# Writing the unshifted scores of a relative attention in four transfers of 32 rows instead of one of 128

## The chip, the cores and the metric

The kernel is one program on one core of a Trainium2 chip. The metric is device time in microseconds (us), from the start of the program to its end, as a median of several executions. Lower is better. Shares of the span are given against one profiled execution.

## The reference

The program is a chain of four layers on a tensor of 8 x 512 tokens of width 128: a plain attention, a causal attention with a mixture of experts, an attention with relative positions, and a low-rank feed-forward layer. The change touches the third. Cut to what matters there:

```python
def _rel_shift(x):
    B, H, Lq, Lr = x.shape
    xp = jnp.concatenate([jnp.zeros((B, H, Lq, 1), x.dtype), x], axis=-1)
    xp = xp.reshape(B, H, Lr + 1, Lq)
    return xp[:, :, 1:].reshape(B, H, Lq, Lr)[..., Lr - Lq:]
...
AC = jnp.einsum('bhid,bhjd->bhij', q + u_bias[None, :, None, :], k)
BD = jnp.einsum('bhid,hjd->bhij', q + v_bias[None, :, None, :], rp)
BD = _rel_shift(BD)
attn = jax.nn.softmax((AC + BD) * scale, axis=-1)
out = jnp.einsum('bhij,bhjd->bhid', attn, v)
```

There are 16 heads of 8 elements and 512 queries and keys. Row i of BD has to be moved sideways by an amount that grows by one from row to row, before it is added to AC.

## The kernel before

The layer is `phase_relative` (line 2260). It runs NI = 32 steps, one for each of 8 sequences and 4 groups of 4 heads. A step holds 16 tiles of 128 queries x 512 keys, in two halves (c = 0 and 1) of HT = 8 tiles; a buffer index s alternates from step to step. For each half:

- TensorE computes the unshifted scores of 8 tiles side by side (`wide_bank`, L2440) and ScalarE copies them from PSUM to SBUF (`copy_wide`, L2519) into `wide[:, s, c, :]`, 128 partitions x CW = 4448 columns of float32. The scores of a tile take W = 544 columns. Row r of the buffer is needed with a shift that depends on r. The four groups of Q = 32 rows are computed with different starts, `start = W * v + P - Q - Q * a` for group a, so that each group fills 8 x 544 = 4352 of the 4448 columns: from column 96 for the first group, 64, 32 and 0 for the others.
- ScalarE's queue issues the transfer `send` (L2524) that writes the buffer to DRAM (`skew`), all 128 rows with all 4448 columns.
- SyncE's queue waits for that write (`sent`) and issues `fetch` (L2353), which reads it back with a row pitch of CW - 1 = 4447, so that each row comes back shifted by one more than the row before: 128 partitions x 4320 columns into `shifted`.
- VectorE adds the content scores that TensorE made in PSUM (L2574) and subtracts the row maximum (L2582), TensorE turns the tile (L2456), ScalarE takes the exponential (L2540), TensorE multiplies with the values (L2469), and ScalarE copies the sums out (L2530).

The order on each engine is written by hand. In step n the wide scores of step n + 2 are made, copied and sent, one bank behind each tile; `send` stands behind tile 7 and tile 15 in ScalarE's order. SyncE's order in a step is: values of the next step, four stores of sums, fetch of half 1 of step n + 1, fetch of half 0 of step n + 2, then the loads of `qu` and `k` and of `qv` (48 partitions each). A fetch waits for its send, and SyncE issues nothing behind it meanwhile. Before ScalarE overwrites `wide[:, s, c, :]` two steps later it waits for the send that read it (L2546). So a half-step, of which there are 64, asks the transfer queues for one send and one fetch, and every second one for three loads on 48 partitions as well.

Of the kernel before, what the change touches and what calls it, by code (L numbers as in the profile page):

```python
# [13 lines left out]
P = 128  # L14
# [7 lines left out]
NI = NB * NG  # L22
# [11 lines left out]
Q = 32  # L34
TG = G * NT
W = L + Q
HT = TG // 2
CW = HT * W + P - Q
# [2221 lines left out]
def phase_relative(nc, sems, qu_stacks, qv_stacks, k_stacks, v9_in, r_stack, ident_in, skew_dram, ctx_out):  # L2260
# [14 lines left out]
    with ExitStack() as ctx:  # L2275
        def sb(name, shape, dt=F32):
            return ctx.enter_context(nc.sbuf_tensor("r_" + name, shape, dt))


        def sem(name):  # L2280
            return sems.new("r_" + name)
# [10 lines left out]
        wide = sb("wide", [P, 2, 2, CW])  # L2292
# [17 lines left out]
        sent = [[sem(f"sent{s}{c}") for c in range(2)] for s in range(2)]  # L2310
# [13 lines left out]
        def steps(step, eng):  # L2324

            for n in range(NI):
                step(n // STEP, n % STEP, n == 0, min(4, NI - 1 - n))

        def uses(it, j):

            return (STEP // 2) * it + j // 2 + 1

        @block.sync
        def _(sp):
            def load(it, j):
                for dst, src in ((qu, qu_stacks), (k, k_stacks)):
                    sp.dma_start(dst[0:SK, j % 2, :, :],
                                 src.rearrange("b r (g h) t -> b g r h t", h=G)[it, j]).then_inc(loaded[j % 2], 16)

            def load_values(it, j):  # L2340
                sp.dma_start(v9[:, j % 2, :, :], v9_in.rearrange("b p t (g v) -> b g p t v", g=NG)[it, j])\
                    .then_inc(v_loaded[j % 2], 16)

            def load_queries(it, j):
                at = ROWS * (j % 2)
                sp.dma_start(qv[at:at + SK, j % 2, :, 0:L], qv_stacks.rearrange("b r (g h) t -> b g r h t", h=G)[it, j])\
                    .then_inc(qv_loaded[j % 2], 16)

            def fetch(it, j, c):

                sp.wait_ge(sent[j % 2][c], 16 * uses(it, j))
                src = skew_dram[j % 2][c]
                sp.dma_start(shifted[:, j % 2, HT * W * c:HT * W * (c + 1) - Q],  # L2353
                             bass.AP(tensor=src.tensor, offset=src.offset + P - 1, ap=[[CW - 1, P], [1, HT * W - Q]]))\
                    .then_inc(skewed[j % 2][c], 16)

            def after(it, j, by):
                return it + (j + by) // STEP, (j + by) % STEP

            def step(it, j, first, left):  # L2360
                n = STEP * it + j
                if left >= 1:
                    sp.wait_ge(head_done, G * n + 2)
                    load_values(*after(it, j, 1))
                if not first:
                    store(n - 1)
                if left >= 1:
                    if not first:
                        sp.wait_ge(keys_ps, TG * n)
                    fetch(*after(it, j, 1), 1)  # L2370
                if left >= 2:
                    sp.wait_ge(keys_ps, TG * n + HT)
                    fetch(*after(it, j, 2), 0)
                if left >= 2:
                    sp.wait_ge(ac_ps, TG * (n + 1))
                    load(*after(it, j, 2))
                if left >= 4:
                    sp.wait_ge(wide_ps, 2 * NBK * (n + 3))
                    load_queries(*after(it, j, 4))

            def store(n):
                sp.wait_ge(out_sb, n + 2)
                for b in range(NT):
                    sp.dma_start(ctx_out[n, :, :, b * P:(b + 1) * P].rearrange("h r i -> r h i"),
                                 osb[Q * b:Q * b + VW, :, :]).then_inc(stored, 16)

            sp.wait_ge(pad_set, 1)
            load_queries(0, 0)
            load_queries(0, 1)
            sp.wait_ge(pad_set, 2)  # L2390
            sp.dma_start(ident[:, :], ident_in).then_inc(consts, 16)
            for s in range(2):
                sp.dma_start(r[ROWS * s:ROWS * s + SK, :, :, :],
                             r_stack.rearrange("r (o g h) t -> g r o h t", g=2, h=G)[s]).then_inc(r_loaded, 16)
            sp.wait_ge(pad_set, 4)
            load(0, 0)
            load_values(0, 0)
            sp.sem_inc(stored, 64)
            for c in range(2):
                fetch(0, 0, c)  # L2400
            sp.wait_ge(wide_ps, 2 * NBK)
            load_queries(0, 2)
            load(0, 1)
            fetch(0, 1, 0)
            sp.wait_ge(wide_ps, 4 * NBK)
            load_queries(0, 3)
            steps(step, sp)
            store(NI - 1)
            for s in range(2):
                sp.wait_ge(loaded[s], 32 * (NI // 2))  # L2410
                sp.wait_ge(v_loaded[s], 16 * (NI // 2))
                sp.wait_ge(qv_loaded[s], 16 * (NI // 2))
                for c in range(2):
                    sp.wait_ge(sent[s][c], 16 * (NI // 2))
                    sp.wait_ge(skewed[s][c], 16 * (NI // 2))
            sp.wait_ge(r_loaded, 32)
            sp.wait_ge(stored, 64 * (NI + 1))
# [96 lines left out]
        @block.scalar  # L2514
        def _(act):
            def copy_wide(n, s, c, bk):
                act.wait_ge(wide_ps, 2 * NBK * n + NBK * c + bk + 1)
                lo, hi = BANK * bk, min(BANK * bk + BANK, CW)
                act.activation(wide[:, s, c, lo:hi], ps_wide[bk % BANKS][:, 0:hi - lo], ACT.Copy).then_inc(wide_sb, 1)  # L2519

            def send(n, s, c):
                act.wait_ge(wide_sb, 2 * NBK * n + NBK * (c + 1))
                dst = skew_dram[s][c]
                act.dma_start(bass.AP(tensor=dst.tensor, offset=dst.offset, ap=[[CW, P], [1, CW]]),  # L2524
                              wide[:, s, c, :]).then_inc(sent[s][c], 16)

            def take_sums(n):
                act.wait_ge(head_done, G * (n + 1) + 2)
                act.wait_ge(stored, 64 * (n + 1))
                act.activation(osb[:, :, :].rearrange("p h i -> p (h i)"), ps_out[:, :], ACT.Copy)\  # L2530
                    .then_inc(out_sb, 1)

            def step(it, j, first, left):
                n, s = STEP * it + j, j % 2
                for u in range(TG):
                    h, b = u // NT, u % NT
                    if b == 0:
                        act.wait_ge(head_done, G * n + h + 1)
                    act.wait_ge(keys_ps, TG * n + u + 1)
                    act.activation(probs[:, h % 2, :, b * P:(b + 1) * P],  # L2540
                                   ps_keys[u % 2][:, :].rearrange("p (j i) -> p j i", j=NT), ACT.Exp,
                                   scale=SCALE).then_inc(exp_done, 1)
                    if left >= 2:
                        c, bk = u // HT, u % HT
                        if bk == 0:
                            act.wait_ge(sent[s][c], 16 * uses(it, j))  # L2546
                        copy_wide(n + 2, s, c, bk)
                        if bk == HT - 1:
                            copy_wide(n + 2, s, c, HT)
                            send(n + 2, s, c)  # L2550
                    if u == 2 and not first:
                        take_sums(n - 1)

            act.sem_inc(exp_done, 2)
            act.sem_inc(out_sb, 1)
            for n in range(2):
                for c in range(2):
                    for bk in range(NBK):
                        copy_wide(n, n, c, bk)
                    send(n, n, c)  # L2560
            steps(step, act)
            take_sums(NI - 1)

# [146 lines left out]
```

## Time and profile before

| | |
|---|---|
| median of 3 runs | 1982.19 us (1959.62 to 1989.26) |
| profiled execution | 1965.66 us, of which span 1963.9 us |
| relative attention in the span | about 961 to 1850 us |
| sends | 64, 2224 KB each |
| fetches | 64, 2160 KB each |

The span is cut into 40 equal slices of 49 us. The relative attention is slices 20 to 37; in the page's second part it shows as the long row of 9s in the line of the transfer engines. The four layers follow each other with a barrier between, so what a half-step gains or loses there is gained or lost at the end.

### The profile page before, as it was taken

What the parts mean: (1) busy time and instruction counts of PE and PEld (TensorE: products, weight loads), DVE (VectorE), ACT (ScalarE), POOL (GpSimd) and SP (SyncE); (2) the same over time, 40 slices, a digit from 0 to 9 for tenths busy, and PEclk for the clock granted to TensorE, in tenths of its full rate; (3) what the DMA queues carried; (4) which work ended last, traced back from release to release, by engine and by line L of the source; (5) the groups of instructions that cost most, each with busy time, mean ns of one, the idle gap of its engine ahead of it and who ended that gap; (6) DMA issues with size and microseconds to landing.
All of it is one profiled execution on the core that took longest, in us unless ns stands there. A gap on an engine that the chain in (4) does not pass through costs nothing. (4 is left out here: it accounts for less than half of the span.)

```text
span 1963.9 us, 48778 instructions
## 1 busy us (share of the span) xinstructions
PE 1356.6 (69%) x18587; PEld 905.4 (46%) x18775; DVE 1171.8 (60%) x3060; ACT 997.9 (51%) x1988; POOL 449.1 (23%) x756
## 2 busy tenths in 40 slices
PE   6636177777745288745248788787888879888657
PEld 3213044444434277622126555565555556555423
DVE  6943477777345223256317676676767667677636
ACT  4424046666611033223147676676767667776333
POOL 5433235555437600087000000000000000000123
PEclk8867579999955589966679999999999999999868
DMA  8439412222031166548799999999999999999422
GB/s 309 171 103 279 103 43 61 69 62 66 21 101 41 43 179 198 160 136 268 203 339 343 370 377 370 379 379 372 384 378 369 368 379 389 379 377 373 136 66 59
DMA packets 174670, 451.83 MB, mean 230 GB/s; under 512 B 41584, under 2 KB 133776, under 8 KB 157360
## 3 DMA queue, kind: packets, MB, share of 16 engines
q1 hardware_dynamic: 130736, 237.53, 36.7%
q10 hardware_dynamic: 31200, 180.04, 23.3%
q0 software_dynamic: 12512, 31.21, 6.0%
q8 instruction: 151, 2.47, 0.5%
q14 instruction: 71, 0.58, 0.1%
HBM read 222.59 MB, written 225.84 MB: 228 GB/s over the span
## 5 line engine op out<-in xcount | busy, mean ns | idle before, releaser
L2574 DVE CUSTOM_DVE_ANT_0 r_shifted<-r_ps_ac,r_shifted 128x512 f32<-128x512 f32 x512 | 352.0, 688 | 264.1 <-PE r_ps_ac L2449 116.7
L2540 ACT ACTIVATE r_probs<-r_ps_keys 128x512 f32<-128x512 f32 x512 | 309.9, 606 | 215.6 <-PE r_ps_keys L2456 189.4
L2519 ACT ACTIVATE r_wide<-r_ps_wide 128x512 f32<-128x512 f32 (+1 forms) x576 | 330.3, 592 | 84.8 <-PE r_ps_wide L2440 84.6
L2456 PE MATMUL r_ps_keys<-r_ident,r_shifted 128*128 128x128 f32 x2048 | 322.1, 281 | 70.8 <-DMA r_k<-stack 24.4
L2456 PEld LDWEIGHTS r_ps_keys<-r_ident,r_shifted 128*128 128x128 f32 x2048 | 264.1, 145 | 62.9 <-issue 21.5
L2440 PE MATMUL r_ps_wide<-r_r,r_qv 128*32 128x96 bf16 (+12 forms) x6144 | 234.8, 253 | 67.7 <-issue 49.9
L2582 DVE TENSOR_SCALAR r_shifted<-r_shifted,r_mx 128x512 f32<-128x512 f32 x512 | 249.3, 487 | 18.3
L926 ACT ACTIVATE c_probs<-c_ps_keys 128x512 f32<-128x512 f32 (+1 forms) x384 | 174.3, 531 | 140.6 <-PE c_ps_keys L852 140.4
L1135 POOL MEMSET n_zeros<- 128x4 f32 x1 | 0.1, 101 | 906.7 <-POOLq L2275 906.7
L2440 PEld LDWEIGHTS r_ps_wide<-r_r,r_qv 128*32 128x32 bf16 x6144 | 103.6, 97 | 164.5 <-issue 163.7
L2469 PE MATMUL r_ps_out<-r_probs,r_v 128*9 128x128 f32 x4096 | 142.4, 274 | 21.1 <-issue 20.4
L989 DVE TENSOR_REDUCE c_mx_off<-c_ps_rows 128x2 f32<-128x768 f32 (+2 forms) x192 | 120.8, 686 | 53.8 <-PE c_ps_rows L823 53.8
L823 PE MATMUL c_ps_rows<-c_qk 48*128 48x128 bf16 (+2 forms) x896 | 75.6, 254 | 90.9 <-DVE c_mx_off L989 43.7
L2449 PE MATMUL r_ps_ac<-r_k,r_qu 128*128 128x512 bf16 x325 | 130.4, 401 | 5.1 <-issue 4.0
L957 POOL TENSOR_SCALAR_AFFINE_SELECT c_probs<-c_probs 128x256 f32<-128x256 f32 x256 | 98.1, 406 | 149.7 <-ACT c_probs L926 149.2
L2469 PEld LDWEIGHTS r_ps_out<-r_probs,r_v 128*9 128x9 f32 x4096 | 105.1, 91 | 31.7 <-issue 27.3
L2449 PEld LDWEIGHTS r_ps_ac<-r_k,r_qu 128*128 128x128 bf16 x512 | 49.1, 96 | 126.0 <-issue 76.6
L1917 POOL DMA_INDIRECT d_y<-expert_out,x_pos x64 | 68.8, 1075 | 167.5 <-issue 167.4
L852 PE MATMUL c_ps_keys<-c_qk 50*128 50x512 bf16 (+3 forms) x512 | 91.2, 305 | 20.5 <-ACT c_probs L926 20.5
L864 PE MATMUL c_ps_out<-c_probs,c_v 128*9 128x128 f32 x2560 | 84.8, 279 | 4.1 <-POOL c_probs L957 4.1
L983 DVE TENSOR_REDUCE c_mx_on<-c_ps_rows 128x8 f32<-128x1024 f32 x64 | 77.7, 1215 | 16.4 <-PE c_ps_rows L831 16.4
L1792 DVE TENSOR_TENSOR e_gu<-e_silu,e_ps_b 128x512 f32<-128x512 f32 x39 | 26.8, 688 | 87.4 <-PE e_ps_b L1718 87.4
(249 smaller groups left out, 1948.8 us busy)
## 6 DMA issues: line engine op xcount, KB each, us to landing
skew<-r_wide ACTq DMA_DIRECT2D x64, 2224.0 KB, 13.6
r_shifted<-skew SPq DMA_DIRECT2D x64, 2160.0 KB, 13.6
by_expert<-a_blank ACTq DMA_DIRECT2D x4, 4352.0 KB
e_w<-in_L_ffn_w_dram SPq DMA_DIRECT2D x117, 128.0 KB, 2.4
c_qk<-qk_stacks POOLq DMA_DIRECT2D x64, 192.0 KB, 3.7
stack<-d_part SPq DMA_DIRECT2D x96, 128.0 KB
qk_stacks<-b_part SPq DMA_DIRECT2D x48, 128.0 KB, 3.5
qk_stacks<-b_part POOLq DMA_DIRECT2D x48, 128.0 KB, 3.7
```

What stands on the lines that cost most here:

```text
L852: last = pe.matmul(ps[:, to:to + WIDTH[j]], qk[at, s, 1, p, j * P:(j + 1) * P], qk[at, s, 0, p, j * P:L], start=True, stop=True, skip_grou ...
L926: act.activation(probs[:, p, e, at:at + width], ps_keys[f % BANKS][:, 0:width], ACT.Exp, scale=SCALE)\
L957: last = pool.affine_select(blocks, blocks, [[0, 2], [1, P]], ALU.is_ge, zero, base=0, channel_multiplier=-1)
L989: last = dve.tensor_reduce(off[:, :, NT * p + b], ps[:, :, at:at + width], AX_X, ALU.max)
L2440: last = pe.matmul(ps[Q * a:Q * a + Q, frm - lo:to - lo], qv[:, s, h, q0 + one:q0 + one + Q], r[:, g // 2, h, at:at + to - frm], start=Tru ...
L2449: pe.matmul(ps_ac[u % 2][:, :], qu[:, s, h, b * P:(b + 1) * P], k[:, s, h, :], start=True, stop=True)\
L2456: last = pe.transpose(ps_keys[u % 2][:, j * P:(j + 1) * P], shifted[:, s, W * u + j * P:W * u + (j + 1) * P], ident[:, :])
L2469: last = pe.matmul(ps_out[Q * b:Q * b + VW, h * P:(h + 1) * P], v9[:, s, j, h * VW:(h + 1) * VW], probs[:, h % 2, j, b * P:(b + 1) * P], s ...
L2519: act.activation(wide[:, s, c, lo:hi], ps_wide[bk % BANKS][:, 0:hi - lo], ACT.Copy).then_inc(wide_sb, 1)
L2540: act.activation(probs[:, h % 2, :, b * P:(b + 1) * P], ps_keys[u % 2][:, :].rearrange("p (j i) -> p j i", j=NT), ACT.Exp, scale=SCALE).th ...
L2574: dve.tensor_tensor_reduce(out=shifted[:, s, W * u:W * u + L], in0=ps_ac[u % 2][:, :], in1=shifted[:, s, W * u:W * u + L], scale=1.0, scal ...
L2582: dve.tensor_scalar(shifted[:, s, W * u:W * u + L], shifted[:, s, W * u:W * u + L], mx[:, u:u + 1], None, ALU.subtract).then_inc(s_ready, 1)
```

## The change

`send` issues four transfers instead of one. Transfer a takes rows 32a to 32a + 31 of the buffer and only the 4352 columns that the group fills. Each adds 16 to the semaphore `sent`, so the three places that wait on it (the fetch, the reuse of `wide`, and the end of the phase) multiply their number by P // Q = 4. What is fetched, and from where in DRAM, is the same.

```diff
@@ fetch
-                sp.wait_ge(sent[j % 2][c], 16 * uses(it, j))
+                sp.wait_ge(sent[j % 2][c], 16 * (P // Q) * uses(it, j))
@@ send
                 act.wait_ge(wide_sb, 2 * NBK * n + NBK * (c + 1))
                 dst = skew_dram[s][c]
-                act.dma_start(bass.AP(tensor=dst.tensor, offset=dst.offset, ap=[[CW, P], [1, CW]]),
-                              wide[:, s, c, :]).then_inc(sent[s][c], 16)
+                for a in range(P // Q):
+                    lo = P - Q - Q * a
+                    act.dma_start(bass.AP(tensor=dst.tensor, offset=dst.offset + Q * a * CW + lo,
+                                          ap=[[CW, Q], [1, HT * W]]),
+                                  wide[Q * a:Q * a + Q, s, c, lo:lo + HT * W]).then_inc(sent[s][c], 16)
@@ step of ScalarE, before the first copy into wide[:, s, c, :]
-                            act.wait_ge(sent[s][c], 16 * uses(it, j))
+                            act.wait_ge(sent[s][c], 16 * (P // Q) * uses(it, j))
```

No engine but ScalarE has other instructions than before. On ScalarE's queue, in the middle of a step (behind tile 7), stood before:

```order
L2540 ACTIVATE r_probs<-r_ps_keys 128x4x128
L2519 ACTIVATE r_wide<-r_ps_wide 128x512
L2519 ACTIVATE r_wide<-r_ps_wide 128x352
L2524 DMA skew_0<-r_wide 128x4448
L2540 ACTIVATE r_probs<-r_ps_keys 128x4x128
```

and now, with the exponential of the next tile (`r_probs`, now L2543) behind four issues:

```order
L2543 ACTIVATE r_probs<-r_ps_keys 128x4x128
L2519 ACTIVATE r_wide<-r_ps_wide 128x512
L2519 ACTIVATE r_wide<-r_ps_wide 128x352
L2526 DMA skew_0<-r_wide 32x4352 x4
L2543 ACTIVATE r_probs<-r_ps_keys 128x4x128
```

The one issue has become four in a row at the same place, here and behind tile 15 (`skew_1`); nothing has changed places.

## Rows read from the trace of the kernel before

**Rows 1.** The page, second part: 40 slices of the span.

```profile
PE   6636177777745288745248788787888879888657
...
DVE  6943477777345223256317676676767667677636
ACT  4424046666611033223147676676767667776333
...
DMA  8439412222031166548799999999999999999422
```

**Rows 2.** Transfers from 1000 to 1800 us: packets, MB, share of 16 engines; issues.

```profile
DMA packets 48940, 299.41 MB, mean 374 GB/s; under 512 B 20285, under 2 KB 30221, under 8 KB 33101
...
q1 hardware_dynamic: 40028, 158.61, 56.6%
q10 hardware_dynamic: 8783, 138.92, 42.7%
q8 instruction: 100, 1.64, 0.9%
...
skew<-r_wide ACTq DMA_DIRECT2D x61, 2224.0 KB, 13.7
r_shifted<-skew SPq DMA_DIRECT2D x61, 2160.0 KB, 13.5
...
r_qu<-stack SPq DMA_DIRECT2D x30, 192.0 KB, 12.8
```

**Rows 3.** Instructions on the tile skew: ns min/median/max, first and last start.

```profile
L2524 ACTq DMA_DIRECT2D skew<-r_wide x64: 325/326/356, 986.5 to 1799.8; - x64
```

**Rows 4.** Waits from 1100 to 1700 us: us in total, times, longest.

```profile
PEld r_ps_wide L2440 <- issue: 95.5, 389, 3.1
...
PE r_ps_keys L2456 <- DMA r_k<-stack: 16.5, 6, 5.9
```

**Rows 5.** Waits of all engines from 1000 to 1800 us.

```profile
DVE r_shifted L2574 <- DMA r_shifted<-skew: 39.9, 2, 38.0
```

**Rows 6.** Waits of SyncE's queue from 1000 to 1800 us.

```profile
SPq L2351 <- DMA skew<-r_wide: 435.0, 44, 21.8
```

**Rows 7.** Stretches: PE, PEld, DVE, ACT, POOL busy; PEclk; DMA share; GB/s.

```profile
970.00:980.00 10.00, 2.46 (x12) 2.06 (x10) 1.16 (x1) 0.00 (x0) 0.00 (x0) 0.50 1.02 150
...
1226.00:1232.00 6.00, 5.68 (x111) 4.18 (x109) 4.59 (x13) 4.98 (x10) 0.00 (x0) 1.00 0.99 417
...
1400.00:1500.00 100.00, 84.61 (x1504) 57.87 (x1530) 69.70 (x184) 69.32 (x134) 0.00 (x0) 0.95 1.00 371
```

**Rows 8.** Instructions on the tile r_r: its loads from DRAM, 48 partitions each.

```profile
L2393 SPq DMA_DIRECT2D r_r<-r_stack x2: 592/616/640, 967.3 to 968.0; - x2
...
DMA to landing us min/median/max: 8.8/11.1/13.4
```

**Rows 9.** Timeline of ScalarE from 15 to 25 us: issues in a row.

```profile
19.25 0.36 ACTq L396 DMA_DIRECT2D by_expert<-a_blank  x1
...
19.64 0.45 ACTq L396 DMA_DIRECT2D by_expert<-a_blank  x1
...
20.12 2.27 ACTq L396 DMA_DIRECT2D by_expert<-a_blank  x2
```

**Rows 10.** Timeline of ScalarE from 1395.4 to 1401.5 us, around a send.

```profile
1396.54 0.33 ACTq L2524 DMA_DIRECT2D skew<-r_wide  x1
1396.97 0.60 ACT L2540 ACTIVATE r_probs<-r_ps_keys 128x512 f32<-128x512 f32 x1 [0.46 <-ACT r_wide L2519]
```

More of the change, by code:

```diff
@@ L2413, in _ @@
                 for c in range(2):
-                    sp.wait_ge(sent[s][c], 16 * (NI // 2))
+                    sp.wait_ge(sent[s][c], 16 * (P // Q) * (NI // 2))
                     sp.wait_ge(skewed[s][c], 16 * (NI // 2))
```

## The prediction

> **What bounds the kernel now.** I read the page's slices first. In the relative attention TensorE stands at 7 or 8 tenths, VectorE and ScalarE at 6 or 7, and the transfer engines at 9 or more throughout [rows 1]. A steady stretch of 100 us says it more sharply: TensorE busy 84.6, VectorE 69.7, ScalarE 69.3, the transfer engines at a share of 1.00 [rows 7]. So the resource without any idle time is the 16 transfer engines.
>
> Next, whether they really set the pace. The 64 sends start from 986.5 to 1799.8 us, one every 813.3 / 63 = 12.9 us [rows 3]. Between 1000 and 1800 us the sends (all of queue q10) take 42.7% of the engines' time: 0.427 x 800 / 61 = 5.60 us of every engine for each send. Queue q1 (the fetches, and all loads and stores) takes 56.6%, which is 7.42 us for each fetch with what goes along [rows 2]. Together 13.0 us: the whole half-step is spent on transfers, one after another on each engine.
>
> Then, who pays. Not VectorE: it waits for `r_shifted` only at the start of the phase, 39.9 us in 2 waits, 38.0 of it one wait [rows 5]. The pressure shows in small waits of TensorE: for `r_k`, 16.5 us in 6 waits in 600 us, and "issue" gaps of up to 3.1 us [rows 4], some of which I take for instructions that arrive late through the same engines (q8, 100 packets, [rows 2]). SyncE spends 435.0 us waiting for sends before fetches [rows 6]; a send lands 13.7 us after its issue and a fetch 13.5 us after [rows 2]. Data sent in one half-step is needed three half-steps later (38.7 us), and 13.7 + 13.5 = 27.2 us are used, so some 11 us of delay per buffer could be absorbed once. A lasting overload of even 2 us per half-step would use that up in six half-steps. Hence I count transfer engine time and nothing else.
>
> **The change part by part.**
>
> Bytes. A send shrinks from 2224 KB to 128 x 4352 x 4 B = 2176 KB, by 2.16%, of 5.60 us: -0.12 us per half-step, -7.5 us over 62 of them (the first two are prologue). DRAM rows stay where they were and the fetch is untouched: 0.
>
> Issues. ScalarE's queue has three more at 0.33 us each [rows 3]: +1.0 us per half-step, ahead of the next exponential. ScalarE is busy for 9.0 of 12.9 us [rows 7], so 3.9 us are idle and it already waits 0.46 us at this place for the copy before [rows 10]. On the path I count 0; the cover is that ScalarE's waits for TensorE shrink by the same amount. Without it the cost would be 62 x 1.0 = 62 us. Behind the issues on that queue are the exponential and the copy of the next tile, for which TensorE waits two tiles later.
>
> Semaphores. Four completion marks per engine instead of one, on packets of a few bytes. The trace has thousands of small packets beside the large ones [rows 2] with no visible price: 0, and at most a few tenths of a us per half-step. The waits have only other numbers; each is met by the last of the four transfers.
>
> Rows on few partitions. This is the term that counts. A transfer over 128 partitions runs at full rate: 417 GB/s at a share of 0.99 from 1226 to 1232 us. From 970 to 980 us only transfers into 48 partitions were served (the two `r_r` loads, then `r_qu` and `r_k`), and the engines were just as busy (1.02) but moved 150 GB/s [rows 7]. The `r_r` loads landed after 8.8 and 13.4 us [rows 8] for 768 KB each, where a send of 2224 KB lands in 13.7. So engine time per byte is 417 / 150 = 2.8 times as long when few partitions take part: the engines meet at the same part of SBUF. A send is now four such transfers, of 32 partitions each. The trace has no large transfer that *reads* SBUF from few partitions, so I bound the factor x on the send's 5.5 us. From below: 1.0, if reads do not collide, or if the four, which together cover all partitions, spread out on the engines; nothing can make it less, since rows on 128 partitions already run at the full 417. From above: 2.8 would hold if all engines met at one group all the time. But every engine alternates between a row of the send and a row of a fetch, which covers 128 partitions, so two engines that meet are in their send rows together about half of the time; half of the excess of 1.8 gives x = 1.9. I take the middle, 1.45, because neither bound has a row of its own kind nearer to it: 0.45 x 5.5 = +2.5 us per half-step, between 0 and +5.0.
>
> The Trainium skill, in "SBUF — State Buffer", section "Door 1: The DMA port swizzle", says that partitions 0 to 31 (like 64 to 95) reach only 8 of the 16 ports over which transfers enter and leave, so that such a transfer gets at most half the rate. By that rule alone the factor would be 2.0 while only sends run and 1.5 in alternation with fetches, and the sum 2.75 - 0.12 = 2.6 us per half-step, an estimate of 2129 us. No run here shows whether it holds for reads of SBUF; that few partitions are slow to write, the stretch from 970 us shows.
>
> **The sum.** 2.5 - 0.12 = +2.4 us per half-step, from 12.9 to 15.3; 62 x 2.4 = +149 us. Against the profiled execution, 1965.66 us, that is 2115 us. The median of the runs shown lies 16 us above that execution, which I leave inside the range.
>
> **The rivals.**
>
> *Reads don't collide.* Then only the bytes count: 1965.7 - 7.5 = 1958 us, and up to 1982 on the level of the median; within 2%. For it: the collision is shown only for writes into SBUF, the four groups cover all partitions between them, and an engine that runs ahead is at another group than its neighbour. Against it: the four are issued in a row, so all engines begin with the same 32 rows, and do so 64 times.
>
> *ScalarE's issues block.* Four issues in a row of large transfers took 0.36, 0.45 and then 2.27 us for two [rows 9]; the third and fourth seem to wait for room. Four sends would then hold ScalarE for 3.08 us instead of 0.33, +2.75, against 3.9 us idle. It decides once ScalarE's idle time is not at the right place: TensorE gets the exponentials late, twice in a step, and up to 62 x 2.75 = 170 us are lost: 2030 (half of it hidden) to 2130 us. For it: those rows are for the same count of 128 partitions and long rows. Against it: they had four times as many rows each, and a half-step of 12.9 us has its slack elsewhere.
>
> *Full collision.* Engines fall in step and stay there, x at 1.9: +5.0 - 0.12 = 4.9 per half-step, 62 x 4.9 = 304, 2269 us.
>
> *Faster by over 2%.* It would need 40 us, five times the whole cut in bytes; only shorter gaps in TensorE, whose instructions and `r_k` come through the same engines, could multiply it. 1925 us; I see nothing that makes them shorter by so much.
>
> **How the numbers follow.** Collision in the middle range (2040 to 2200 us): 0.44. Full collision (above 2200): 0.12. Blocking issues without collision: 0.08. Reads don't collide: 0.33. Faster by over 2%: 0.03. 2% is about what a measurement of this kernel can tell from no change. Slower by over 2% has 0.44 + 0.12 + 0.08 = 0.64; within 2%, 0.33; faster, 0.03. Since cases of both kinds hold much of the chance, the range must reach from the byte-only case, 1950 us, to 2240 us; it leaves out faster and the top of the full collision. The likeliest case by itself spans 2040 to 2200.
>
> **What the new profile would show.** If I am right: starts of the sends 15 us apart instead of 12.9; the share of the transfer engines still 1.0 but fewer than 374 GB/s, about 310; q10's share of engine time up from 42.7% to about 52% with 2% fewer bytes, so that a send takes some 8 us of each engine; landing of a send up from 13.7 us; TensorE's busy share down with VectorE waiting for `r_shifted` in the steady state, where it does not now. If reads do not collide: 374 GB/s and q10's share as now, a send at 5.5 us per engine. If issues block: the four issues take far more than 1.3 us together, ScalarE waits fewer us for TensorE, TensorE waits for ScalarE, and the transfer engines fall below 1.0. The forecast fails if the collision is smaller than a tenth in x (then 0.5 us per half-step, 30 us in all), or if SyncE's fetch, which now starts later behind its send, leaves engines idle.

## The result and the profile after

The changed kernel takes 2133.45 us (median of 6 runs, 2129.1 to 2144.38), the kernel before 1979.02 us beside it. The ratio is 1.081, with a 95% interval of 1.077 to 1.085: 8% slower. The profiled execution has a span of 2132.3 us.

The page's slices of the changed kernel, which answer to [rows 1]:

```profile
PE   6543477777442884543588787877777877777747
...
DVE  6932777774342332641456565565666655565636
ACT  4422066666220331333365565655555655555333
...
DMA  8257222221311664787998899899999999999512
```

The phase is longer, every engine has fewer tenths, and the transfer engines are no longer at 9 all along: there are 8s in what was a plain row of 9s. The stretch of 100 us that stands in [rows 7] for the kernel before reads now (columns as there):

```profile
1400.00:1500.00 100.00, 81.77 (x1349) 52.79 (x1347) 61.23 (x159) 58.47 (x113) 0.00 (x0) 0.88 0.94 307
```

The transfer share is 0.94 instead of 1.00 and 307 GB/s are moved instead of 371. The transfers from 1000 to 1800 us, beside [rows 2]:

```profile
q1 hardware_dynamic: 33528, 132.34, 49.8%
q10 hardware_dynamic: 9861, 114.44, 43.5%
...
skew<-r_wide ACTq DMA_DIRECT2D x205, 544.0 KB, 11.1
```

In 800 us there are 205 / 4 = 51 sends where there were 61. A send takes 0.435 x 800 / 51.25 = 6.79 us of each engine, up from 5.60 although it has 2.2% fewer bytes: for its bytes 1.24 times as long. That is the size the collision would have, half of the forecast one. But the two queues together fill 93.3% only, so engine time alone does not set the pace any more. The issues on the tile skew, beside [rows 3]:

```profile
L2526 ACTq DMA_DIRECT2D skew<-r_wide x256: 308/574/3827, 985.3 to 1967.9; - x128
```

The longest issue is 3.8 us, where all 64 stood between 325 and 356 ns. From first to last, less the 4 us within the last group, a half-step takes (1967.9 - 985.3 - 4) / 63 = 15.5 us; it was 12.9. What a group of four does to ScalarE shows in its timeline (start, duration, line, idle before):

```profile
1403.95 0.95 ACT L2519 ACTIVATE r_wide<-r_ps_wide 128x512 f32<-128x512 f32 x2
1404.93 3.69 ACTq L2526 DMA_DIRECT2D skew<-r_wide  x4
1408.72 0.60 ACT L2543 ACTIVATE r_probs<-r_ps_keys 128x512 f32<-128x512 f32 x1 [3.82 <-issue]
...
1419.38 5.46 ACTq L2526 DMA_DIRECT2D skew<-r_wide  x4
1424.94 0.60 ACT L2543 ACTIVATE r_probs<-r_ps_keys 128x512 f32<-128x512 f32 x1 [5.59 <-issue]
```

Before the next exponential ScalarE is idle for 3.8 and 5.6 us, where it was 0.46 us in [rows 10]. These two groups are no exception: over the phase (without its first two sends) a group of four takes 4.6 us on average and 7.3 at most, from the start of its first issue to the end of its last. And TensorE now waits for the exponential. The waits from 1100 to 1700 us of the changed kernel (in total, times, longest):

```profile
ACT r_probs L2543 <- issue: 153.6, 30, 7.5
PE r_ps_keys L2456 <- ACT r_probs L2543: 103.2, 38, 5.8
...
ACT r_probs L2543 <- PE r_ps_keys L2456: 57.0, 84, 2.3
```

and the answering ones of the kernel before, same stretch:

```profile
ACT r_probs L2540 <- PE r_ps_keys L2456: 133.3, 122, 7.2
...
PE r_ps_keys L2456 <- ACT r_probs L2540: 0.2, 1, 0.2
```

Read the pairs against each other. Before, ScalarE waited for TensorE; now TensorE waits 103.2 us in 600 for the exponential, and ScalarE 153.6 us for its own queue.

TensorE's granted clock fell too (columns as in [rows 7]; first the kernel before, then three stretches of the changed one):

```profile
1000.00:1800.00 800.00, 654.69 (x11875) 450.21 (x12044) 548.44 (x1448) 552.19 (x1059) 0.00 (x0) 0.95 1.00 374
```

```profile
1000.00:1800.00 800.00, 619.55 (x10024) 394.82 (x10025) 459.61 (x1194) 455.44 (x884) 0.00 (x0) 0.87 0.94 310
1408.00:1410.00 2.00, 0.54 (x3) 0.57 (x4) 0.67 (x3) 1.28 (x3) 0.00 (x0) 0.82 1.00 417
1410.00:1412.00 2.00, 2.00 (x19) 1.18 (x18) 0.17 (x1) 2.00 (x5) 0.00 (x0) 0.50 1.02 416
```

Behind the group of issues at 1404.93 us TensorE is busy for 0.54 of 2 us, and then works at half of its full clock, 1.2 GHz instead of 2.4. Its busy time per half-step went from 654.69 / 800 x 12.9 = 10.6 us to 619.55 / 800 x 15.5 = 12.0 us. Waiting for the exponential adds 103.2 / 600 x 15.5 = 2.7 us; the two are 14.7 of the 15.5 us. So a part of what a stall costs may be the slower clock behind it. No run here holds the clock still, so that part is not separated in what follows.

So after the change there were two candidates: rows on few partitions (theory C), and ScalarE held by its issues (theory I). Both were in the prediction, the second with a chance of 0.08.

### The profile page after: what moved, and what is told of

It reads as the page before. It is cut to its first block and busy times, and to the rows that moved or that the text cites. A ratio compares the mean times of both kernels' runs of the same rounds, so it can differ in the third digit from the quotient of the medians.

```text
span 2132.3 us, 49158 instructions
## 1 busy us (share of the span) xinstructions
PE 1446.7 (68%) x18775; PEld 930.7 (44%) x18775; DVE 1179.6 (55%) x3060; ACT 992.2 (47%) x1988; POOL 450.4 (21%) x756
## 5 line engine op out<-in xcount | busy, mean ns | idle before, releaser
L2543 ACT ACTIVATE r_probs<-r_ps_keys 128x512 f32<-128x512 f32 x512 | 313.9, 613 | 396.9 <-issue 243.9
L2456 PE MATMUL r_ps_keys<-r_ident,r_shifted 128*128 128x128 f32 x2048 | 356.4, 303 | 170.1 <-ACT r_probs L2543 166.5
L2456 PEld LDWEIGHTS r_ps_keys<-r_ident,r_shifted 128*128 128x128 f32 x2048 | 283.3, 157 | 235.9 <-issue 174.6
L2440 PE MATMUL r_ps_wide<-r_r,r_qv 128*32 128x96 bf16 (+12 forms) x6144 | 244.8, 268 | 58.6 <-issue 29.7
L2449 PE MATMUL r_ps_ac<-r_k,r_qu 128*128 128x512 bf16 x512 | 218.3, 427 | 2.5 <-issue 1.3
L983 DVE TENSOR_REDUCE c_mx_on<-c_ps_rows 128x8 f32<-128x1024 f32 x64 | 77.8, 1215 | 16.5 <-PE c_ps_rows L831 16.5
L864 PEld LDWEIGHTS c_ps_out<-c_probs,c_v 128*9 128x9 f32 x2560 | 66.1, 93 | 20.6 <-issue 15.0
```

Source lines behind the costliest of these rows:

```text
L864: last = pe.matmul(ps_out[32 * i:32 * i + VW, at * P:(at + 1) * P], v9[:, s, j, h * VW:(h + 1) * VW], probs[:, p, e, OFF[j] + (b - j) * P: ...
L2440: last = pe.matmul(ps[Q * a:Q * a + Q, frm - lo:to - lo], qv[:, s, h, q0 + one:q0 + one + Q], r[:, g // 2, h, at:at + to - frm], start=Tru ...
L2449: pe.matmul(ps_ac[u % 2][:, :], qu[:, s, h, b * P:(b + 1) * P], k[:, s, h, :], start=True, stop=True)\
L2456: last = pe.transpose(ps_keys[u % 2][:, j * P:(j + 1) * P], shifted[:, s, W * u + j * P:W * u + (j + 1) * P], ident[:, :])
L2543: act.activation(probs[:, h % 2, :, b * P:(b + 1) * P], ps_keys[u % 2][:, :].rearrange("p (j i) -> p j i", j=NT), ACT.Exp, scale=SCALE).th ...
```

## The experiments

All times are medians; ratios are to runs of the kernel before on the same chip. "Half-step" is the distance of sends, by the first and last start as above; "engine time" is the send's queue share from 1000 to 1800 us, times 800 us, divided by the sends in that stretch.

| run | ratio [95%] | half-step, us | engine time of a send, us |
|---|---|---|---|
| before | 1 | 12.9 | 5.60 |
| the change | 1.081 [1.077, 1.085] | 15.5 | 6.79 |
| strided4 | 1.030 [1.021, 1.038] | 13.9 | 5.70 |
| full_columns | 1.087 [1.081, 1.094] | 15.6 | 6.96 |
| pool_one | 1.004 [0.999, 1.008] | 13.0 | 5.65 |
| pool_four | 1.039 [1.032, 1.046] | 14.2 | 6.85 |
| pool_strided4 | 0.997 [0.993, 1.000] | 13.1 | 5.65 |
| pool_two64 | 1.050 [1.040, 1.061] | 14.6 | 7.25 |
| spread_issues | 1.035 [1.028, 1.042] | 14.1 | 6.47 |
| scalar_held | 1.105 [1.098, 1.113] | 16.3 | 5.45 |
| held_short | 1.014 [1.007, 1.020] | 13.3 | 5.53 |
| extra_bytes | 1.026 [1.019, 1.032] | 13.8 | 6.76 |

**strided4: four transfers, each spread over all partitions.**

```diff
                 for a in range(P // Q):
-                    lo = P - Q - Q * a
-                    act.dma_start(bass.AP(tensor=dst.tensor, offset=dst.offset + Q * a * CW + lo,
-                                          ap=[[CW, Q], [1, HT * W]]),
-                                  wide[Q * a:Q * a + Q, s, c, lo:lo + HT * W]).then_inc(sent[s][c], 16)
+                    act.dma_start(bass.AP(tensor=dst.tensor, offset=dst.offset + a * CW,
+                                          ap=[[(P // Q) * CW, Q], [1, CW]]),
+                                  wide[a:P:P // Q, s, c, :]).then_inc(sent[s][c], 16)
```

> Four transfers per send as after the change, but transfer a takes rows a, a+4, a+8, ... with all 4448 columns, so each of the four is spread over all partitions (the result stays the same). Theory C (collision: rows of few neighbouring partitions cost engine time): the cost goes, about 1980 to 2000 us, a send at 5.6 us of each engine as before. Theory I (ScalarE is held by four issues in a row, 4.5 us instead of 0.33): the cost stays, 2090 to 2140 us, the four issues still take over 4 us.

2031.42 us: between the two, and neither theory alone. Its transfers and its issues:

```profile
q10 hardware_dynamic: 10938, 129.90, 40.6%
...
skew<-r_wide ACTq DMA_DIRECT2D x228, 556.0 KB, 9.7
```

```profile
L2525 ACTq DMA_DIRECT2D skew<-r_wide x256: 454/626/2421, 986.5 to 1866.5; - x128
```

A send is back at 0.406 x 800 / 57 = 5.70 us of engine time: the collision is gone. What is left, 3%, points at ScalarE's queue. A group of four issues takes 3.2 us on average instead of 4.6, still far from 0.33, and TensorE's wait for the exponential is in between, too. From its waits, 1100 to 1700 us:

```profile
PE r_ps_keys L2456 <- ACT r_probs L2542: 45.4, 47, 3.1
```

**full_columns: 32 neighbouring rows, all 4448 columns.**

```diff
-                    lo = P - Q - Q * a
-                    act.dma_start(bass.AP(tensor=dst.tensor, offset=dst.offset + Q * a * CW + lo,
-                                          ap=[[CW, Q], [1, HT * W]]),
-                                  wide[Q * a:Q * a + Q, s, c, lo:lo + HT * W]).then_inc(sent[s][c], 16)
+                    act.dma_start(bass.AP(tensor=dst.tensor, offset=dst.offset + Q * a * CW,
+                                          ap=[[CW, Q], [1, CW]]),
+                                  wide[Q * a:Q * a + Q, s, c, :]).then_inc(sent[s][c], 16)
```

> Four transfers of 32 neighbouring rows as after the change, but each with all 4448 columns. Both theories: the time of the changed kernel plus at most the 2% of bytes, 2133 to 2145 us. A bigger step would say that the shorter or shifted rows matter by themselves.

2145.3 us, at the upper end of what was expected; 1.087 against 1.081. The cut in bytes would be worth some 0.5%, but the intervals overlap. The cost isn't in the shortened rows.

**pool_four and pool_one: the same transfers, issued by GpSimd.** `send` moves to a queue that is empty in this phase; ScalarE issues nothing.

```diff
+        @block.gpsimd
+        def _(pool):
+            for n in range(NI):
+                for c in range(2):
+                    send(pool, n, n % 2, c)
...
-                            send(n + 2, s, c)
```

> The four transfers of the change, issued from GpSimd's queue, which does nothing else in this phase; ScalarE issues none. Theory C: the collision stays, 2080 to 2140 us. Theory I: ScalarE is free again, 1965 to 1995 us, with ScalarE's waits before the exponential after a send gone.

> The one transfer of the kernel before, issued from GpSimd's queue: the control of the run with four on that queue. Both theories: 1965 to 1995 us, as before, unless that queue itself costs something.

pool_one, 1978.09 us, shows that the queue itself costs nothing measurable. pool_four, 2047.57 us, keeps about half of the loss; it lies between the ranges of the two theories, so neither alone had the size right. Its transfers, and TensorE's wait for the exponential in it:

```profile
q1 hardware_dynamic: 36272, 143.87, 51.3%
q0 software_dynamic: 10760, 124.86, 47.1%
...
skew<-r_wide POOLq DMA_DIRECT2D x220, 544.0 KB, 10.1
```

```profile
PE r_ps_keys L2456 <- ACT r_probs L2549: 1.0, 4, 0.3
```

The wait is gone (1.0 us in 600), the engines are full again (51.3 + 47.1 = 98.4%), and a send takes 0.471 x 800 / 55 = 6.85 us. This is theory C by itself: 1.2 us more per send, 1.2 us more per half-step (14.2 against 13.0, both against pool_one).

**pool_strided4: both causes away, four transfers kept.** The transfers of strided4 on the queue of pool_one.

> Four transfers of rows a, a+4, a+8, ... with all 4448 columns, issued from GpSimd's queue: neither neighbouring rows nor issues on ScalarE are left, only the number of transfers. If these two are the whole cost: 1970 to 1995 us, a send at 5.5 us of each engine. If the number of transfers costs something by itself (completion marks, starts): 2000 us or more.

1974.23 us, ratio 0.997. The number of transfers costs nothing by itself. With it the square is complete: neither cause 0.997, issues only 1.030, collision only 1.039 (with the cut columns), both 1.081. The two together cost about as much as one on top of the other: 1.030 x 1.039 / 0.997 = 1.073 against 1.081, and with intervals of up to 0.8% on each the rest isn't resolved. The issue times do differ: a group of four takes 3.2 us on average in strided4, and 4.6 and 4.4 us where the rows are neighbours (the changed kernel and full_columns).

**pool_two64: two transfers of 64 rows from GpSimd.** Shown against pool_four; the waits on `sent` count two transfers instead of four.

```diff
-                for a in range(P // Q):
+                for a in range(2):
...
+                                          ap=[[CW, 64], [1, CW]]),
+                                  wide[64 * a:64 * a + 64, s, c, :]).then_inc(sent[s][c], 16)
```

> Two transfers of 64 neighbouring rows with all 4448 columns, from GpSimd's queue. If 64 neighbouring partitions are served by no more ports than 32 are (the Trainium skill, SBUF page), the collision is as large as with four of 32: 2035 to 2060 us. If the cost falls with the number of partitions in a transfer: 1995 to 2025 us.

2081.35 us, above both ranges. The engine time of a send, 0.485 x 800 / 53.5 = 7.25 us:

```profile
q0 software_dynamic: 8799, 125.24, 48.5%
...
skew<-r_wide POOLq DMA_DIRECT2D x107, 1112.0 KB, 12.8
```

Twice as many neighbouring partitions don't halve the cost; it is at least as large (1.28 times pool_one, against 1.24 for four of 32, by bytes). By the Trainium skill, "SBUF — State Buffer", section "Door 1: The DMA port swizzle", 64 neighbouring partitions reach no more ports than 32. The run agrees in this, for reads of SBUF: two of 64 cost no less than four of 32. The ports themselves stand in no trace here.

**spread_issues: the four issues one tile apart, on ScalarE.**

```diff
-            def send(n, s, c):
+            def send(n, s, c, groups=range(P // Q)):
...
-                for a in range(P // Q):
+                for a in groups:
...
-                            send(n + 2, s, c)
+                            send(n + 2, s, c, (0,))
+                    if u % HT < P // Q - 1 and (left >= 2 if u >= HT else left >= 1 and not first):
+                        if u >= HT:
+                            send(n + 2, s, 0, (u % HT + 1,))
+                        else:
+                            send(n + 1, 1 - s, 1, (u + 1,))
```

> The four transfers of the change on ScalarE's queue, but one behind tile 7 (15) and one each behind the exponentials and copies of the next three tiles, instead of four in a row. Theory: an issue is slow because it stands right behind the one before; spread, the four take about 1.3 to 2 us together and only the collision is left: 2040 to 2070 us. If each issue waits for the engines whatever its place: 2100 to 2140 us as after the change.

2044.46 us, as pool_four (1.035 against 1.039, the intervals overlap): ScalarE issues as many transfers as in the changed kernel and loses nothing by it. The expectation for the time holds, its reason only partly. From the timeline:

```profile
1410.28 0.31 ACTq L2526 DMA_DIRECT2D skew<-r_wide  x1
...
1411.01 1.54 ACTq L2526 DMA_DIRECT2D skew<-r_wide  x1
1411.14 0.61 ACT L2543 ACTIVATE r_probs<-r_ps_keys 128x512 f32<-128x512 f32 x1
1411.62 0.62 ACT L2519 ACTIVATE r_wide<-r_ps_wide 128x512 f32<-128x512 f32 x1
```

Issues still last up to 2.9 us, 1.54 here, and the four of a send 3.1 us together on average, not the 1.3 to 2 us that were expected. But the exponential and the copy at 1411.14 and 1411.62 us run while the issue lasts. In the changed kernel the two copies of 1403.95 us end at 1404.90, the four issues begin at 1404.93, and nothing runs beside them. TensorE's wait is 11.3 us instead of 103.2:

```profile
PE r_ps_keys L2456 <- ACT r_probs L2543: 11.3, 28, 1.1
```

**scalar_held and held_short: the time on ScalarE by itself.** The kernel before, and idle copies of a constant into a spare tile behind each send, nine or three. (Two waits at the start of the phase, not shown, see to it that the constant is there.)

```diff
+                for i in range(9):
+                    act.activation(dump[:, i, :], r[:, 0, 0, 0:BANK], ACT.Copy)
```

> The kernel before with its one transfer, and nine idle copies of 128x512 on ScalarE behind each send, some 4.3 us, as long as the four issues hold it: the price of holding ScalarE alone, with no transfer changed. From the strided run (2.8 us more holding, +0.8 us per half-step) I expect +1.1 to 1.5 us per half-step: 2040 to 2070 us. If holding costs only beside transfers that are slower: within 10 us of 1975.

> As the run that holds ScalarE, with three idle copies of 128x512 instead of nine: 1.6 us instead of 4.8. With nine the half-step is 16.5 us, so ScalarE's chain without any holding would take 16.5 - 4.8 = 11.7, and with 1.6 us 13.3 us, just over the 12.94 us of the transfers: 1985 to 2010 us. If every us of holding costs 0.76 us as with nine: +75 us, 2050 us.

scalar_held took 2188.72 us, far above the expected 2040 to 2070: holding ScalarE for 4.8 us costs 3.4 us per half-step, not 1.5. The expectation took the strided run's price per us, although the first of the time held is covered; that was a wrong way to scale. held_short, with 1.6 us, took 1998.09 us, as expected: 0.4 us per half-step, so some 1.2 us of the 1.6 were covered. (The 16.5 us in its expectation is scalar_held's half-step without the first sends of the phase; from first to last it is 16.3.) The stretch from 1000 to 1800 us of scalar_held (columns as in [rows 7]):

```profile
1000.00:1800.00 800.00, 591.33 (x9350) 393.71 (x9489) 432.72 (x1119) 665.00 (x1276) 0.00 (x0) 0.81 0.83 298
```

The engines fall to 0.83 and ScalarE is busy for 665 of 800 us. TensorE's clock is down to 0.81, and its busy time per half-step is 591.33 / 800 x 16.3 = 12.0 us, as in the changed kernel, with no transfer changed. So the 3.4 us are the price of holding ScalarE with what it does to TensorE's clock. Together with the strided run and the change the points lie roughly on one line: half-step = 11.3 us plus the time held, unless the transfers take longer. 11.3 + 1.6 = 12.9 (13.3 measured), 11.3 + 2.9 = 14.2 (strided4, 13.9 measured), 11.3 + 4.3 = 15.6 (the change, 15.5 measured), 11.3 + 4.8 = 16.1 (16.3 measured); 2.9 and 4.3 are the average groups of 3.2 and 4.6 us less the 0.33 of one issue. The 11.3 is fitted to these runs and not seen in any row, and misses by up to 0.4 us, as much as the whole loss of held_short.

**extra_bytes: engine time by itself.** A second transfer of 128 rows x 888 columns behind the one of pool_one, into a spare place. The fetch waits for both.

> One transfer per send from GpSimd's queue, and behind it a second of 128 rows x 888 columns into a spare place of DRAM (read by nobody): 20% more bytes, by 5.5 us per send +1.1 us of each engine per half-step, which is what the collision of the four groups added (46.9% of 14.17 us against 42.3% of 13.02 us), with no neighbouring rows and ScalarE free. If engine time sets the pace, the half-step grows by the same 1.1 us and the run takes 2040 to 2055 us. If there is cover for it, 1975 to 2000 us.

2026.33 us, between the two ranges: most of the added engine time shows, but less than expected. The engine time of the pair grew as planned, 0.490 x 800 / 58 = 6.76 us, +1.1, and the half-step by 0.75 only (13.8 against 13.0):

```profile
q1 hardware_dynamic: 36677, 146.63, 50.8%
q0 software_dynamic: 13083, 159.69, 49.0%
```

Here q1, the fetches and loads, takes 0.508 x 13.8 = 7.0 us per half-step, 0.3 less than with pool_one (0.563 x 13.0 = 7.3). That accounts for most of the difference. Why q1 got cheaper beside a longer send was not tried.

## Why the prediction came out

2115 us were forecast and 2133 measured, but the working was right in one half only.

- **What bounds the kernel** (13.0 us of engine time per half-step): held. More engine time lengthened the half-step in pool_four and pool_two64 one for one, and in extra_bytes by two thirds.
- **Bytes**, -0.12 us: not resolved. full_columns against the change, 1.087 against 1.081, has the right sign and size.
- **Semaphores and number of transfers**, 0: held (pool_strided4, 0.997).
- **Rows on few partitions**, +2.5 us with x = 1.45: the mechanism is right, the term was mis-sized. It measured x = 1.24 and +1.2 us with ScalarE free. The upper bound, 2.8 from loads into 48 partitions, lay far off, and the middle between the bounds was twice too high. By the rule of the Trainium skill that the prediction names ("SBUF — State Buffer", section "Door 1: The DMA port swizzle") it estimated 1.5, which was twice too high as well.
- **Issues**, "On the path I count 0": this is the step that failed. The price of an issue, 0.33 us, was read from sends that never stood behind another; four in a row took 3.69 and 5.46 us in the timeline. The cover was read as an average, 3.9 of 12.9 us idle, and held_short shows that 1.6 us already cost 0.4. In the runs the four issues take 4.6 us on average instead of 1.3, and the loss comes with TensorE waiting 103.2 us in 600 for the exponential and its granted clock down from 0.95 to 0.87; the clock was no term of the prediction. The right rows were there, [rows 9], and the rival made of them put the loss at up to 2.75 us per half-step. (Its lower time, 2030 us for half of the loss hidden, is a slip: 1965.7 + 85 - 7.5 is 2043 us.) On its own (strided4) the cost is 1.0 us, and on top of the collision 15.5 - 14.2 = 1.3 us.
- So the forecast +2.4 us per half-step was really +1.2 of collision and +1.3 of holding: 62 x 2.5 = 155 us, and 154 were measured. That the number was right is luck: a term twice too large stood in for one put at nothing.
- **What the new profile would show**: the half-step (15 forecast, 15.5 measured) and 310 GB/s came. The engine time of 8 us (6.8 measured), q10's share of 52% (43.5), a full share of 1.0 (0.94) and VectorE waiting for `r_shifted` did not come; the marks of the rival did, over 1.3 us for four issues, TensorE waiting for ScalarE, and a share below 1.0. The forecast held the rival to come instead of the collision; the two came together.

## What to carry to other kernels

Cutting a transfer into pieces by neighbouring partitions costs engine time if the engines are full, and rows taken in strides over all partitions do not; 2% fewer bytes do not pay for it. Price an issue by what stands before it on its queue: several large ones in a row stall the compute engine that issues them, and a queue without other work, or a tile of work between issues, takes that cost away. An average idle share is no cover for a block of several us in a chain that goes from engine to engine at every tile, and where the block stalls TensorE, look at its granted clock behind it as well.

## What the runs showed that was not expected

- Every fourth row (strided4, pool_strided4) costs the same engine time as all rows at once, 5.70 and 5.65 us against 5.60, although each such transfer also has 32 partitions only. It is the neighbourhood, not the number.
- An issue on ScalarE's queue takes from 0.31 to 3.8 us (256 issues in the changed kernel), and on GpSimd's, for the same transfers, 0.49 to 0.73 us:

```profile
L2519 POOL DMA_DIRECT2D skew<-r_wide x256: 489/492/734, 984.5 to 1881.5; - x128
```

  What a long issue waits for wasn't isolated. That it is room for the transfers behind those still under way would fit the groups of four, 4.6 and 4.4 us with neighbouring rows and 3.2 with strided ones, and is only argued.
- No version beat the kernel before by more than the intervals: pool_strided4 at 0.997 [0.993, 1.000] is the lowest.
